# Attention inside a post-norm attention and expert layer: step 14 turned into the score buffers' upper banks, value projection one slot earlier, weights loaded first, copies ahead of query rounding

## The reference

```
latent_kv = x @ w_kv_down                     # 256 -> 128
k, v = split(latent_kv @ w_kv_up)             # 16 heads of 64 each
q = x @ w_q                                   # 16 heads of 64
att = softmax(where(causal, q k^T / 8, -inf)) # per head, 1024 x 1024
y = att v
x = layernorm(x + y @ w_out)
```

## Time and profile before

| what | us |
|---|---|
| runs (three) | 3440.41, 3443.92, 3446.7 |
| the profiled execution's own time | 3441.83 |
| its span (first to last instruction of the program) | 3440.1 |
| PE busy, share of the span | 3158.1 (92%) |
| DVE, ACT, POOL busy | 2091.6, 1853.1, 1374.7 |
| attention stage in the trace, about | 90 to 2270 |
| granted clock of PE, mean over the span | 0.965 |

### The profile page before, as it was taken

How to read it: one execution, slowest core, us unless ns; L and a number is a source line. 1 busy time by engine, 2 the same in 40 slices (tenths; PEclk the granted TensorE clock), 3 DMA queues, 4 the chain that set the end, 5 groups by cost and what they waited for, 6 DMA issues and landing times. The chain is left out here.

```text
span 3440.1 us, 69338 instructions
## 1 busy us (share of the span) xinstructions
PE 3158.1 (92%) x20382; PEld 2509.7 (73%) x20382; DVE 2091.6 (61%) x5849; ACT 1853.1 (54%) x4063; POOL 1374.7 (40%) x1543
## 2 busy tenths in 40 slices
PE   5999999999999999999999999979926999999995
PEld 2776676777676767676767677669925999999995
DVE  1666666666666666666656666656675545555555
ACT  2666666666666666666656666633302434333435
POOL 0334333334343334333433333322213656545655
PEclk7999999999999999999999999989957999999998
DMA  6444344445444444444444444347612333323327
GB/s 206 99 114 113 90 112 113 105 102 118 102 106 111 109 99 114 105 103 111 108 100 114 108 101 110 89 185 265 232 49 54 72 71 75 63 41 70 75 55 207
DMA packets 184390, 376.22 MB, mean 109 GB/s; under 512 B 23873, under 2 KB 108225, under 8 KB 181953
## 3 DMA queue, kind: packets, MB, share of 16 engines
q1 hardware_dynamic: 153152, 316.91, 35.7%
q0 software_dynamic: 29696, 50.48, 7.4%
q10 hardware_dynamic: 1152, 4.19, 0.3%
HBM read 123.97 MB, written 79.76 MB: 59 GB/s over the span
## 5 line engine op out<-in xcount | busy, mean ns | idle before, releaser
L242 POOL TENSOR_SCALAR prob<-prob,inv 128x128 f32<-128x128 f32 (+7 forms) x1024 | 770.6, 753 | 1319.4 <-DVE inv L590 1319.4
L585 DVE CUSTOM_DVE_ANT_0 s_ps<-s_ps,mask 128x128 f32<-128x128 f32 (+7 forms) x1024 | 781.4, 763 | 728.0 <-PE s_ps L368 723.6
L493 ACT ACTIVATE prob<-s_ps,neg_max 128x128 f32<-128x128 f32 (+7 forms) x1024 | 759.0, 741 | 256.4 <-DVE neg_max L585 243.9
L377 PE MATMUL t_ps<-ident,prob 128*128 128x128 f32 x4608 | 691.8, 276 | 27.0 <-ACT prob_t L571 24.0
L367 PE MATMUL s_ps<-k_hh,q_hl 128*128 128x512 f32 (+3 forms) x1536 | 595.3, 388 | 57.8 <-ACT prob L493 36.5
L571 ACT ACTIVATE prob_t<-t_ps 128x512 f32<-128x512 f32 (+3 forms) x768 | 415.1, 541 | 355.2 <-PE t_ps L377 354.4
L377 PEld LDWEIGHTS t_ps<-ident,prob 128*128 128x128 f32 x4608 | 532.8, 141 | 98.3 <-ACT prob_t L571 37.6
L393 PE MATMUL o_ps<-prob_t,v 128*64 128x512 f32 (+3 forms) x3072 | 537.5, 492 | 1.5 <-DVE y L607 1.5
L368 PE MATMUL s_ps<-k_lz,q_hl 128*128 128x512 f32 (+3 forms) x1536 | 517.2, 349 | 0.0
L367 PEld LDWEIGHTS s_ps<-k_hh,q_hl 128*128 128x128 f32 x1536 | 291.3, 190 | 212.3 <-issue 95.9
L393 PEld LDWEIGHTS o_ps<-prob_t,v 128*64 128x64 f32 x3072 | 204.0, 136 | 284.9 <-issue 266.2
(11 more groups left out here) (153 smaller groups left out, 5349.4 us busy)
## 6 DMA issues: line engine op xcount, KB each, us to landing
k_hh<-k_high SPq DMA_DIRECT2D x256, 256.0 KB, 4.5
q_hl<-q_high SPq DMA_DIRECT2D x128, 256.0 KB, 3.6
q_hl<-q_low SPq DMA_DIRECT2D x128, 256.0 KB, 4.2
k_lz<-k_low SPq DMA_DIRECT2D x128, 256.0 KB, 5.0
y_d<-y SPq DMA_DIRECT2D x128, 256.0 KB, 3.9
c_yt<-y_d SPq DMA_DIRECT2D x16, 2048.0 KB, 8.2
w_raw<-w SPq DMA_DIRECT2D x16, 1024.0 KB, 7.4
a_xt<-x_t SPq DMA_DIRECT2D x8, 1024.0 KB, 9.5
```

What stands on the lines that cost most here:

```text
L242: pool.tensor_scalar(pr, pr, inv[:, s % 4:s % 4 + 1], 1.0, ALU.mult, ALU.mult).then_inc(norm_done, 1)
L377: mm = pe.transpose(t_ps[k % 2][:, j * P:(j + 1) * P], prob[s % 4][:, (first + j) * P:(first + j + 1) * P], ident[:])
L493: act.activation(prob[s % 4][:, 0:(q + 1) * P], s_ps[s % 2][:, 0:(q + 1) * P], ACT.Exp, scale=-1.0, bias=neg_max[:, s % 4:s % 4 + 1], accu ...
L585: dve.tensor_tensor_reduce(part, part, mask[:, T - (q + 1) * P:T], 1.0, -MASKED, ALU.add, ALU.min, neg_max[:, s % 4:s % 4 + 1]).then_inc(m ...
```

## The change

Four edits, all in the attention stage.

1. Step 14's two chunks are transposed into columns 512 to 1023 of the score buffers (`turned_in`) instead of `t_ps`. PE waits for `exp_done` of step 15 there in place of `copied`; step 15, which still uses `t_ps`, waits for one copy fewer. ACT and DVE copy step 14 from the same place.
2. `V_AT` is (7, 9) instead of (8, 10); ACT's copies of the values go with it to slots 8 and 10.
3. In SP's turn the load of weights stands ahead of the store of y's first half and of the placing of queries.
4. In ACT's slot 13 the rounding of queries stands behind the copy of step 13.

```diff
-    Q_AT, K_AT, V_AT = (12, 15), (2, 5), (8, 10)
+    Q_AT, K_AT, V_AT = (12, 15), (2, 5), (7, 9)
...
+        def turned_in(s, k):
+            return s_ps[k % 2][:, HALF:T] if s == 14 else t_ps[k % 2][:]
...
                     load_latent(b + 1)
+                if weights:
+                    sp.wait_ge(proj_done, 6 * n + 12)
+                    sp.sem_inc(passed, 1)
+                    load_weights((m + 3) & (NPAIR - 1), 1 - u)
                 store_y(b, m, 0)
                 if keys:
                     place_queries(n + 2, u)
-                if weights:
-                    sp.wait_ge(proj_done, 6 * n + 12)
-                    sp.sem_inc(passed, 1)
-                    load_weights((m + 3) & (NPAIR - 1), 1 - u)
                 if keys:
                     place_keys(n + 2, u)
                 store_y(b, m, 1)
...
             def turn(n, s):
                 pe.wait_ge(norm_done, 16 * n + s + 1)
+                if s == 14:
+                    pe.wait_ge(exp_done, 16 * n + 16)
                 for k, first, count in chunks(s):
-                    pe.wait_ge(copied[k % 2], CH // 2 * n + k // 2)
+                    if s == 15:
+                        pe.wait_ge(copied[k % 2], CH // 2 * n + k // 2 - 1)
+                    elif s != 14:
+                        pe.wait_ge(copied[k % 2], CH // 2 * n + k // 2)
                     for j in range(count):
-                        mm = pe.transpose(t_ps[k % 2][:, j * P:(j + 1) * P],
+                        mm = pe.transpose(turned_in(s, k)[:, j * P:(j + 1) * P],
...
                     if s == W_SPLIT and after >= 2:
                         weights_high(n + 2, u)
-                    if s - 1 in Q_AT and after >= 2:
-                        high(n + 2, u, Q_AT.index(s - 1))
                     if s == 0 and after:
                         high(n + 1, 1 - u, 1)
...
-                                           t_ps[0][:, 0:count * P].rearrange("p (j c) -> p j c", c=P),
+                                           turned_in(s, k)[:, 0:count * P].rearrange("p (j c) -> p j c", c=P),
                                            ACT.Copy).then_inc(copied[0], 1)
+                    if s - 1 in Q_AT and after >= 2:
+                        high(n + 2, u, Q_AT.index(s - 1))
...
-                                            t_ps[1][:, 0:count * P].rearrange("p (j c) -> p j c", c=P)
+                                            turned_in(s, k)[:, 0:count * P].rearrange("p (j c) -> p j c", c=P)
                                             ).then_inc(copied[1], 1)
```

More of the change, by code:

```diff
@@ L318, in turn @@
                     load_latent(b + 1)
-                store_y(b, m, 0)
-                if keys:
-                    place_queries(n + 2, u)
                 if weights:
@@ L326, in turn @@
                     load_weights((m + 3) & (NPAIR - 1), 1 - u)
+                store_y(b, m, 0)
+                if keys:
+                    place_queries(n + 2, u)
                 if keys:
```

## The result

The changed kernel takes 3380.54 us at the median of four runs (3378.71 to 3380.80), the kernel before 3443.74 us beside it, so 63 us less. The ratio is 0.9817, 95% interval 0.9803 to 0.9832. The prediction was 3383 us with a range of 3354 to 3402.

A forecast was written before the change was run, and what follows sets the result against it. PE, busy 92% of the span, was taken to bound the kernel, so only its short stops could shrink: (0.18 + 0.60) x 63 = 49.1 us plus 11 us, 60 us, giving 3383 us, range 3354 to 3402.

The forecast's parts named there:

- The sum: Whole kernel: 0.18 + 0.60 us in 63 pairs, 49.1 us, plus 11 us for weights first, gives 60 us.
- Stop A: Slot 8: PE's scores wait for an exponential, 1532.71; the values' first half, moved to slot 7, fills it.
- The new stop at slot 12: Slot 12's scores wait 3.60 us from slot 10's, through maximum, exponential and read-out; 0.38 us of the gain lost.
- R1: Rival: the chain at slot 12 does not bind; gain 0.46 instead of 0.18 us, 3366 us; chance 0.13.
- the 0.17 us of slot 13: Distance from slot 13's two score matmuls to its transposes, taken for slot 14 too: transposes at 1511.55 instead of 1512.15.
- stop B: Slot 14: transposes start 0.77 us after the scores, behind ACT's copy of step 13, late because ACT rounded queries first.
- The rule on banks: Values share the keys' bank in slot 7; by rotation alone, moving them exposes the rounding and the sum keeps only 0.08.
- R2: Rival: the value move gains nothing (11 us) or slot 14 half (19 us); 3394 to 3413, around 3399; chance 0.18.
- R3: Rival: ACT freed of its 1.50 us wait removes small lags in slots 5 to 8; 13 us, 3370; chance 0.13.
- R4: Rival: keys arrive late at slot 13, weights being right behind them; 3472 at 2.5 us delay, about 3628 at 5.0; chance 0.05.
- R5: Rival: step 14's copies hold the score buffers so PE waits; given nothing of its own, would look like R2.
- Loop branch: PE stops seven times 2.87 us at slot 8; same gain taken there, give or take 1 us each, 7 us in all.

The follow-up runs named there:

- run 6: Changed kernel, but ACT copies the second half of the values in slot 11, behind the exponential of step 13: 3380.11 us, pair 32.53 us.
- run 7: Changed kernel, but step 13's mask and maximum cover only the last 512 of its 896 columns: 3365.05 us, pair 32.23 us.
- run 9: Changed kernel with both step 13's maximum over the last 512 columns and the values' second half copied in slot 11: 3362.38 us, pair 32.13 us.
- run 8: Changed kernel, but the values' second half is split, two blocks in slot 9 and two in slot 10, copied in slot 11: 3368.76 us.
- run 1: Changed kernel with the values back in slots 8 and 10, all else as changed: 3394.26 us, pair 32.77 us.
- run 4: Changed kernel with step 14 back through `t_ps` and the query rounding again ahead of the copy: 3426.81 us, pair 33.22 us.
- run 3: Changed kernel with step 14 back through `t_ps`, ACT's new order kept: 3408.83 us, pair 32.92 us.
- run 5: Changed kernel with ACT again rounding queries ahead of the copy of step 13, step 14 still in the score buffers: 3383.44 us.
- run 2: Changed kernel with the weights again loaded behind the placing of queries: 3397.47 us, normal pair 32.49 us.
- run 10: Changed kernel with every load of weights issued a second time, into tiles nobody reads: 3379.97 us, pair 32.53 us.

## Why the prediction was right

**The sum.** It had 60 us; the profiled executions differ by 61.0: 65.7 in the attention stage, less 0.8 before it and 3.9 behind it. The stages behind are unchanged; span less the end of the attention stage gives 1171.9 to 1177.5 us for them in the traces above, so the last is their spread. That 60 and 61.0 are so close is in part luck: the stage gained 5.7 us more than the sum had, and the spread behind it took 3.9 back. Of the 5.7, 1.9 are the normal pair (0.81 us for 0.78) and 1.7 the 14 pairs of edit 3 (0.91 for 0.80). Another 1.3 fell between the first scores and pair 0's slot 0, at a granted clock of 0.67 instead of 0.50 from 80 to 90 us, and is not traced to an edit. The rest is scattered.

**Edit 2: right, by its working.** Stop A is filled, the values wait for DVE, and 9.38 us from slot 7 to slot 12 are 0.16 under the old 9.54 (0.18 was taken). The new stop at slot 12 and its 3.60 us chain are as forecast; runs 6, 7 and 9 tell the chain from ACT's order, and run 8 from any stop with a length of its own. Undersized: slot 12 itself lost a lag of 0.10 us, so the edit is worth 0.24 us (run 1). Rival R1 falls.

**Edits 1 and 4: the sum right, the reading thin.** 0.60 was taken; slot 14's transposes gained 0.51 between the kernels, all from slot 14 to 15 0.55, and undoing both costs 0.69 (run 4). The 0.09 too much came from the 0.17 us of slot 13: slot 14's two score matmuls start 0.14 us apart, slot 13's 0.06, in the kernel before as well (1511.38 and 1511.52, 1510.50 and 1510.56). That POOL and the exponential are next, and that the added wait costs nothing, holds: from slot 14's second score matmul to its transposes it is 0.11 us, in slot 13 it is 0.12. The cause given for stop B, ACT's order, was less than half of it: 0.30 us beside the other edits, and the other 0.39 is the 1.31 us that one bank needs between two uses (run 3). In the kernel before it was less still: the copy started at 1511.50, and 0.66 us behind its transposes would have been 1510.67 + 0.66 = 1511.33, so the order cost 0.17 us there, an estimate. By the same estimate edit 4 alone would have gained 0.17 us there, not 0.60. That the two pay once between them, and that edit 4 adds nothing to edit 1, was right (run 5).

**Edit 3: right.** 11 us taken; 12 us in the 14 pairs named (run 2), though the whole run lost 17.

**The rule on banks.** The prediction's estimate was 0.1 us of waiting for the keys' rounding in a normal pair, and it is only that. In m = 6, where DVE has x to split first, the values wait 0.56 us for it, which the prediction did not price. DVE in slot 6 of such a pair:

```profile
294.01 0.67 DVE L626 TENSOR_TENSOR b_xt_lo<-b_xt,b_xt_hi 128x512 fp32r<-128x512 f32 x1
294.60 0.68 DVE L614 TENSOR_TENSOR k_low<-j_ps,k_high 128x512 fp32r<-128x512 f32 x1
```

The low part of the keys comes 0.6 us later, behind the split, and so do the values: the 0.59 us that m = 6 keeps. This is read from the rows and not tried by a run. But edit 2 did not make m = 6 slower: with the values back in slot 8 (run 1) that pair is 0.61 us over its neighbours too, for another wait. There ACT's split of x stands ahead of the rounding and the copy, and slot 8's scores wait for the exponential behind them, 0.86 us where a normal pair has 0.34:

```profile
1626.86 0.62 ACT L534 ACTIVATE b_xt_hi<-b_xt 128x512 fp32r<-128x512 f32 x1
...
1629.28 0.50 PE L373 MATMUL s_ps<-k_hh,q_hl 128*128 128x512 f32 x1 [0.86 <-ACT prob L505]
```

So the edit fills that longer stop in m = 6, and the wait for the bank takes its place; whether another bank for the values would save the 0.59 us is not shown. In run 3, where one bank costs 0.39 us a pair, the trace agrees with the rule that independent groups should rotate through banks (the Trainium skill, Perfetto Trace Analysis, "Matmuls").

**R2 to R5.** R2's halves are excluded by runs 1 and 4. R3 falls: slots 5 and 6 kept their length. R4 had no price: from the last key DMA's landing to slot 13 the slack was 1.4 us at the median and 0.9 at the least, and is now 0.9 and 0.4. The exception is one pair of the last batch, where PE waits 0.29 us for a key DMA. With the weights behind them the keys land 0.2 us later, not 1 or more. That little is delayed fits the ring order (the Trainium skill, DMA: Bandwidth & Descriptors, "Queues, rings and completion order"); run 10 adds little, as said there. R5 falls: slots 15 and 0 to 6 kept their length to 0.02 us.

**Loop branch.** PE stops for it six times in the kernel before, 2.39 to 2.87 us, not seven times 2.87; the seventh pass leaves the loop without such a stop. The six pairs took 36.0 to 38.4 us before and 35.2 to 37.7 after, 224.3 and 220.9 together: 0.57 us gained each on average, near the 0.78 taken. Single pairs moved by +1.6 to -3.0 us, more than the 1 us allowed each, and this cancelled in the sum.

## What to carry to other kernels

When a stop of the busiest engine ends on a chain of other engines, add the chain up start to start: it tells where the stop reappears once the work is moved, and how much work must be put between its two ends. For a stop that ends on a copy, ask first when the copy's data come, and only then what stands before it on its engine; a reordering helps only down to the round trip through the buffer, and another buffer helps past it. Two edits against one stop must be undone one by one and together, since either may hide the other.

## What the runs showed of the hardware that I had not expected

One PSUM bank of transposes takes 1.31 us from the start of one group of four 128 x 128 blocks to the start of the next through the same bank: 0.66 until ACT starts to copy, 0.60 for the copy, 0.05 back (run 3). PE's own four blocks take about 0.40 of that, an estimate from seven blocks in 0.70 us (1588.22 to 1588.92). With three weight DMAs issued from 3.1 us (median) behind the last key DMA of a pair, on the same queue and while it is still under way, that DMA lands after 5.8 us at the median, against 5.6 without them.
